# Normed rows of groups 1 and 2 shared by two engines, and VectorE's queue reordered, in a fused transformer block

## The reference

```python
def rmsnorm(x, w):
    return x * jax.lax.rsqrt(jnp.mean(x * x, axis=-1, keepdims=True) + EPS) * w

def film(x, cond, w, b):
    scale, shift = jnp.split(cond @ w + b, 2, axis=-1)
    return x * (1.0 + scale[:, None, :]) + shift[:, None, :]

x_in = x
h = film(rmsnorm(x, norm1_w), cond, film1_w, film1_b)
Q = h @ q_w + q_b
K = h @ k_w + k_b
V = h @ v_w + v_b
scores = jnp.einsum('bnd,bmd->bnm', Q, K) * D ** (-0.5)
out = jnp.einsum('bnm,bmd->bnd', softmax(scores), V)
x = x_in + (out @ proj_w + proj_b)
x_in = x
h = film(rmsnorm(x, norm2_w), cond, film2_w, film2_b)
return x_in + gelu(h @ mlp_w1 + mlp_b1, approximate=False) @ mlp_w2 + mlp_b2
```

## Time and profile before

| | |
|---|---|
| time, median of 3 runs | 229.41 us (229.32 to 229.54) |
| time of the profiled execution | 229.15 us |
| its span in the profile | 227.3 us |
| TensorE busy | 215.9 us (95%) |
| VectorE busy | 151.2 us (67%) |
| ScalarE busy | 111.3 us (49%) |
| GpSimd busy | 72.3 us (32%) |
| granted TensorE clock, mean | 0.999 of full speed |

### The profile page before, as it was taken

One profiled execution on the slowest core, in us unless ns is written; L12 is line 12 of the kernel. 1 busy time (PEld: TensorE's weight loads), 2 busy tenths in 40 slices (PEclk: granted clock), 3 DMA queues, 4 the chain that ended last, 5 costly groups with the idle time before them and its releaser, 6 DMA issues.

```text
span 227.3 us, 3461 instructions
## 1 busy us (share of the span) xinstructions
PE 215.9 (95%) x1260; PEld 188.9 (83%) x1260; DVE 151.2 (67%) x291; ACT 111.3 (49%) x207; POOL 72.3 (32%) x102
## 2 busy tenths in 40 slices
PE   0998999998999999999999999999999999999994
PEld 0777888886999999999999999888788878889993
DVE  0599866588799988899989973148524852446222
ACT  3167655246333355433368860494449444644440
POOL 1575753000565315752445316046004500200000
PEclk9999999999999999999999999999999999999999
DMA  5994001037857887653565462000610061002002
GB/s 168 342 413 188 3 0 46 0 134 241 273 191 229 232 261 233 213 197 132 173 221 205 140 198 72 3 0 0 230 49 0 8 219 51 3 0 92 0 3 92
DMA packets 18017, 29.86 MB, mean 131 GB/s; under 512 B 2128, under 2 KB 12112, under 8 KB 17872
## 3 DMA queue, kind: packets, MB, share of 16 engines
q1 hardware_dynamic: 15696, 21.25, 29.5%
q10 hardware_dynamic: 2304, 8.39, 9.7%
HBM read 17.58 MB, written 12.06 MB: 130 GB/s over the span
## 4 chain that ended last, share of the span: by engine, by line
PE 80%; DVE 9%; DMA 6%; SPq 2%; issue 1%; ACT 1%; DVEq 0%
PE psum L764 35%; PE psum L838 20%; PE psum L893 9%; PE psum L885 5%; PE psum L891 5%; DMA raw<-in_film_wT_dram 3%; PE psum L782 3%; DMA keys_first<-crossing 2%; PE psum L776 2%; DMA crossing<-turned 1%; PE psum L756 1%; DVE x_rows L729 1%; SPq L194 1%; DVE V_all L554 1%; PE psum L890 1%
## 5 line engine op out<-in xcount | busy, mean ns | idle before, releaser
L710 DVE TENSOR_TENSOR G_all<-probs,G_all 128x512 fp32r<-128x512 f32 x32 | 22.5, 713 | 44.4 <-ACT G_all L489 44.4
L838 PEld LDWEIGHTS psum<-V_all,probsT 128*128 128x128 f32 x384 | 47.4, 188 | 2.6 <-DVE probsT L658 1.4
L764 PE MATMUL psum<-hT,w 128*128 128x512 f32 x192 | 49.1, 392 | 0.0
L838 PE MATMUL psum<-V_all,probsT 128*128 128x256 f32 x384 | 48.0, 281 | 1.0 <-DVE probsT L658 1.0
L764 PE MATMUL psum<-hT,G_all 128*128 128x512 f32 x192 | 46.5, 392 | 0.0
L489 ACT ACTIVATE probs<-psum,vcol 128x512 f32<-128x512 f32 x32 | 22.0, 688 | 44.9 <-PE psum L764 44.4
L764 PEld LDWEIGHTS psum<-hT,w 128*128 128x128 f32 x192 | 35.5, 188 | 6.8
L764 PEld LDWEIGHTS psum<-hT,G_all 128*128 128x128 f32 x192 | 35.1, 188 | 7.0
L430 ACT CAST probsT<-keys_first 128x1024 fp32r<-128x1024 f32 x16 | 16.8, 1049 | 34.7 <-DVE raw L651 15.2
L335 POOL TENSOR_TENSOR x_rows<-x_rows,add_row 128x256 f32<-128x256 f32 x16 | 11.8, 740 | 63.9 <-DVE probsT L658 63.9
L893 PE MATMUL psum<-w,G_all 128*128 128x512 f32 x84 | 30.6, 398 | 0.0
(11 more groups left out here) (72 smaller groups left out, 258.1 us busy)
## 6 DMA issues: line engine op xcount, KB each, us to landing
keys_first<-crossing SPq DMA_DIRECT2D x64, 128.0 KB, 3.1
crossing<-turned ACTq DMA_DIRECT2D x8, 512.0 KB, 3.9
crossing<-raw ACTq DMA_DIRECT2D x8, 512.0 KB, 3.7
out_dram<-x_rows SPq DMA_DIRECT2D x7, 256.0 KB, 3.1
x_rows<-in_x_dram SPq DMA_DIRECT2D x3, 512.0 KB, 9.0
rows_crossing<-raw SPq DMA_DIRECT2D x3, 512.0 KB, 2.6
raw<-rows_crossing SPq DMA_DIRECT2D x12, 128.0 KB, 2.8
raw<-in_film_wT_dram SPq DMA_DIRECT2D x2, 512.0 KB, 8.3
```

The costliest lines, as they stand in the source:

```text
L710: dve.tensor_tensor(gelu[:, m, LO, :], gelu_full[:, m % 2, :], gelu[:, m, HI, :].bitcast(F32), ALU.subtract).then_inc(gelu_ready, 1)
L764: last = pe.matmul(dst, stationary(a, k), moving(b, k), start=(n == len(tiles) * len(PASSES) - 1), stop=(n == 0))
L838: last = pe.matmul(bank(6 + t % 2, D), probsT[:, t % 2, a, k, :], V_all[:, t // KT * KT + k, s, :], start=(n == 0), stop=(n == KT * len(PA ...
```

## The change

Six edits. GpSimd norms two of the four rows of groups 1 and 2 (before: three and four), VectorE the other two. On VectorE, the scaling of the bias products and the normed rows of group 1 come ahead of the low part of `vp_w`, and `squares(2)` right behind that. The film products and coefficients of the second batch, until now ahead of `low_G(0)`, go behind it, in between and behind group 1's low columns; VectorE's rows of group 2 follow them. TensorE's wait for `add_row` goes from the first to the fourth tile of V's first projection. SyncE loads x's group 2 ahead of the two output biases.

```diff
             load(bias_rows[:, :, :], rows[B:B + 2, :].partition_broadcast(P), k_in)
+            load_x(2)
             load(add_row[:, :, :], out_bias.partition_broadcast(P), rows_in)
-            load_x(2)
             load_x(3)
...
                 pool.wait_ge(xT_done, g)
-                normed_rows(g, range(GT if g > 1 else GT - 1))
+                normed_rows(g, range(GT if g > 2 else GT // 2))
...
+            dve.wait_ge(bias_ready, DT + 1)
+            dve.tensor_scalar(small[:, 0:DT + 1], small[:, 0:DT + 1], SCALE, None, ALU.mult).then_inc(bias_scaled, 1)
+            dve.wait_ge(xT_done, 1)
+            normed_rows(1, GT, range(GT // 2, GT))
             dve.wait_ge(vp_hi, 1)
             dve.tensor_tensor(vp_w[:, LO, :, 0:D], bank(6).rearrange("p (t n) -> p t n", t=DT),
                               vp_w[:, HI, :, 0:D].bitcast(F32), ALU.subtract).then_inc(vp_ready, 1)
-            dve.wait_ge(xT_done, 1)
-            normed_rows(1, GT, range(GT - 1, GT))
+            squares(2)
             dve.wait_ge(addrow_done, 1)
             dve.wait_ge(rows_in, 16)
             dve.tensor_tensor(add_row[:, 0, :], bank(7, D), add_row[:, 0, :], ALU.add).then_inc(addrow_ready, 1)
-            dve.wait_ge(bias_ready, DT + 1)
-            dve.tensor_scalar(small[:, 0:DT + 1], small[:, 0:DT + 1], SCALE, None, ALU.mult).then_inc(bias_scaled, 1)
             dve.wait_ge(bias_scaled, 1)
...
-            film_products(0, 1, late_place)
-            coefficients(0, 1)
-            squares(2)
             low_G(0)
             for g in range(1, GROUPS):
-                low_columns(g, slice(g * GW, (g + 1) * GW))
+                tokens = slice(g * GW, (g + 1) * GW)
+                low_columns(g, tokens, (0,))
+                if g == 1:
+                    film_products(0, 1, late_place, (0,))
+                low_columns(g, tokens, (1,))
+                if g == 1:
+                    film_products(0, 1, late_place, range(1, 2 * DT))
+                    coefficients(0, 1)
+                    dve.wait_ge(xT_done, 2)
+                    normed_rows(2, 2 * GT, range(GT // 2, GT))
                 low_V(g - 1)
                 group_terms(g - 1)
                 if g == 1:
...
                         if j == 0:
                             pe.wait_ge(key_terms, g)
+                    elif j == GT - 1:
+                        pe.wait_ge(addrow_ready, 1)
...
                     pe.wait_ge(vp_ready, 1)
-                    pe.wait_ge(addrow_ready, 1)
```

## The result

The changed kernel took 229.99 us (median of 22 runs) against 229.53 us for the kernel before on the same chip: ratio 1.002, interval 1.0011 to 1.0029, so slower by 0.25 to 0.67 us, 0.46 at the middle. The forecast was a loss of 1.0 us (230.4); its range, 229.25 to 231.0, holds the measured time.

The account below looks back on a forecast made before the run. TensorE, busy 95% of the span, was taken as the bound. VectorE's terms summed to 1.26 us later for `squares(3)`; after 0.25 us of slack, a loss of 1.0 us, hence 230.4 us, range 229.25 to 231.0.

Parts of the forecast that it names:

- The lead at group 1: TensorE's second half of G for group 1 about 0.8 us earlier, gone once V of group 1 waits for `key_terms`.
- The sum for VectorE: All delays and savings on VectorE ahead of `squares(3)`, together making it end 1.26 us later, at about 26.93.
- the first pair: VectorE's two normed rows of group 1, beside GpSimd's two: +0.51 us, lower bound +0.03.
- rival (1): Larger loss: costlier meetings with GpSimd, 231.0 us, or group 1's row halves in series, 230.8 us; chance 0.14.
- The second pair: VectorE's two normed rows of group 2, behind the film products: +0.78 us, bounds 0.54 and 1.02.
- The squares: VectorE's `squares(2)` and `squares(3)` no longer running beside GpSimd's work: -0.43 and -0.17 us.
- The low columns of group 1: VectorE's first low column meeting GpSimd's second high column: +0.40 us, lower bound 0 if VectorE comes first.
- the film products: On VectorE, now beside GpSimd's roots and rows; one of four meets a row: +0.17 us, bounds 0 and 0.51.
- The slack: 0.25 us between `squares(3)` and TensorE's start at 29.35: GpSimd's wait for ScalarE before group 2's high columns.
- with the same 1.82 us: GpSimd's high columns of group 2 keep their duration, so TensorE starts group 2 at 30.35, not 29.35.
- rival (3): Faster by over 0.25 us: VectorE's low column does not stop group 2's second high column; 228.65 us, chance 0.08.
- theory A: Added rows keep VectorE from `squares(3)`; through GpSimd's program order that holds up group 2's high columns.

## Why the prediction came out as it did

The sign, the place and the mechanism were right: VectorE is late with `squares(3)`, GpSimd's roots of group 3 wait for it, the high columns wait for the roots and TensorE for the columns; with the squares on ScalarE, which cuts this path, the loss is gone, and with the roots behind the columns most of it. The lead at group 1 (0.80) and its end at `key_terms` (forecast 26.2 in the old trace's time; 26.09, or 26.31 when moved by 0.22) came as written.

**The size was not right**: 0.46 of the 1.0 us came. That the range held the time says little for it, since it reached from a gain of 0.16 to a loss of 1.6. The prediction named a start of group 2's projection before 29.5 as the sign of being wrong. It was 29.43 in its own trace and 29.65 when moved by the 0.22, so the sign lay on the edge; the idle time ahead of it was 0.22, not 0.7 to 1.0. And what said why was not what the prediction had named, VectorE's rows and low column, but GpSimd's high columns.

**The sum for VectorE** was 1.26 and measured 1.18. That it came so near is luck in part, by errors that cancel. In steps from start to start: the first pair took 0.92 in place of 0.51, +0.41 (forecast +0.51); in series, as in rival (1), the pair would have ended at 17.79 in the old trace's time, and it ended at 17.40. The second pair was forecast at +0.78. Its rows took 0.54 (23.87 to 24.41), but the two coefficients ahead of them, with 0.25 of idle time behind, took 0.71 (23.16 to 23.87) in place of 0.27, so +0.98. The idle time stands in all five traces that have both pairs and this order; in the three where the rows came at another moment it does not. The first row started beside GpSimd's second (23.59 to 24.07), so this may be a meeting that shows as idle time; no run tests it. The squares made -0.46 and -0.19, near the forecast -0.43 and -0.17. The low columns of group 1 were forecast at +0.40 and made +0.01: VectorE came first (20.04, GpSimd's second high column 20.05), and the first film product paid instead, 0.83 us: the film products made +0.40, where +0.17 stood. The rest is +0.03.

**The slack** of 0.25 was right: the first high column is 0.91 later by offset (28.07 - 15.62 against 27.38 - 15.84), which is 1.18 less 0.27.

**The step that failed** is "with the same 1.82 us" for the high columns, the term that made the loss 1.0. They took 1.21, because both of ScalarE's columns had long been there and GpSimd ran its two without a gap. That is the mechanism of rival (3), which the prediction set aside with "VectorE will wait there as before": it does wait, but GpSimd no longer does, and so VectorE comes second. It returned 0.61 of the 0.91 us and left a loss of 0.30 at the projection. Behind it 0.15 more was lost, as the low columns took 1.69: the second half, whose weight load waited 0.32 us for them, is 0.35 late and the next transposes 0.45.

**A reading that failed without changing the forecast**: "no idle time" behind 29.35, and with it 1.42 us as all there is to win. The weight load's 0.26 of unexplained idle time was a wait for high columns. Unhindered, a projection follows V's start after 2.96 us, not 3.21, so the kernel before was already 0.25 late in groups 2 and 3. This is why two versions came out faster than the accounts of theory A.

## What to carry to other kernels

Work moved onto an engine whose queue is full was paid at the last thing in that queue that somebody waits for; look for it first, and see whether that one can move (here two squares, to an engine that was idle). Where two engines hand on pieces and disturb each other, ask who is released first: a later start can turn a meeting round and change both durations. And a row of matmuls without idle time can hide a wait; compare the weight loads and the step between starts with the same pair of stages elsewhere.

## What the runs showed of the hardware

An instruction of VectorE or GpSimd that meets one of the other engine is shown as a longer instruction: 0.62 to 1.16 us for a high column, 0.69 to 1.09 for a low one, 0.41 to 0.83 for a film product. (Whether the 0.25 us of idle time ahead of VectorE's second pair is such a meeting too stays open.) Which of the two is stretched went with starts 0.01 to 0.07 us apart. In the kernel before VectorE started at 28.03 and GpSimd at 28.04, and GpSimd's column was the longer. In the changed kernel it was 28.66 for GpSimd and 28.73 for VectorE, and in the run where a single wait turned it 28.45 and 28.52; there VectorE's was the longer. The Trainium skill, "SBUF — State Buffer", section "SBUF: two separate sides", says that of a GpSimd instruction and a VectorE instruction with two SBUF inputs (the low column is one), whichever starts first gets the shared port pair for the whole instruction and the other fully blocks. The order of who is stretched agrees with that. The amount agrees less for the normed rows of group 1: VectorE's two took 1.00 us beside GpSimd's two, which took 0.96, and all four ran from 16.07 to 17.18, 1.11 us, where one behind the other would take about 1.50 (an estimate, 2 x 0.48 + 2 x 0.27 from the rows). What part of an instruction overlaps, the runs do not show.
